# Last two attentions of a four-block kernel: the query projection with tokens on partitions, TensorE turning the result, ScalarE summing the squares

## What is computed

```python
# attention three: 16 query heads, 4 key heads of width 128, queries from x, keys and values from ctx (64 tokens each)
q = rmsnorm(x @ Wq + bq) * qn_w          # per head: q * rsqrt(mean(q*q) + 1e-6)
k = rmsnorm(ctx @ Wk + bk) * kn_w
out = softmax(q @ k.T / sqrt(128) + mask) @ (ctx @ Wv + bv) @ Wo
# attention four: the same heads, keys and values from ctx and x together (128 tokens), rotary positions
q = rope(rmsnorm(x @ Wq.T) * q_norm_w, pos_q)
k = rope(rmsnorm(concat(ctx, x) @ Wk.T) * k_norm_w, pos_k)
out = softmax(q @ k.T / sqrt(128)) @ v @ Wo.T
```

## Time and profile before

| what | value |
|---|---|
| median of three runs | 1300.43 us |
| the profiled execution: time / span | 1304.3 us / 1302.5 us |
| TensorE, VectorE, ScalarE, GpSimd busy | 88%, 65%, 48%, 27% of the span |
| attention three, first projection to the last output projection | 513.5 to about 735 us |
| attention four, the same | 968.9 to about 1222 us |
| share of the chain that ended last: TensorE, VectorE, ScalarE | 65%, 18%, 5% |

### The profile page before, as it was taken

How to read it: one execution, slowest core, us unless ns; L and a number is a source line. 1 busy time by engine, 2 the same in 40 slices (tenths; PEclk the granted TensorE clock), 3 DMA queues, 4 the chain that set the end, 5 groups by cost and what they waited for, 6 DMA issues and landing times.

```text
span 1302.5 us, 22884 instructions
## 1 busy us (share of the span) xinstructions
PE 1147.4 (88%) x8124; PEld 844.3 (65%) x8147; DVE 850.5 (65%) x1920; ACT 621.5 (48%) x1407; POOL 352.9 (27%) x328
## 2 busy tenths in 40 slices
PE   4867869999969999899999988888998999999894
PEld 3554644444455665889988746666657888898753
DVE  7788966888867663455546585333497777775664
ACT  5575435677733343344433422222266766666252
POOL 0040011222121002222222146566422433334032
PEclk8756976999969999899999889899999999999998
DMA  7010034000032235000000262522371000000100
GB/s 257 2 44 1 1 137 203 1 2 2 2 134 91 88 140 174 1 2 1 1 1 1 92 288 84 196 85 86 101 289 66 17 18 17 17 9 9 49 1 33
DMA packets 44571, 89.30 MB, mean 69 GB/s; under 512 B 7280, under 2 KB 30448, under 8 KB 42672
## 3 DMA queue, kind: packets, MB, share of 16 engines
q1 hardware_dynamic: 39184, 73.45, 15.7%
q0 software_dynamic: 5280, 14.42, 3.4%
HBM read 68.72 MB, written 21.10 MB: 69 GB/s over the span
## 4 chain that ended last, share of the span: by engine, by line
PE 65%; DVE 18%; issue 6%; ACT 5%; DMA 2%; POOL 2%; SPq 1%; another core or an unknown queue 1%; DVEq 0%; ACTq 0%; POOLq 0%; PEldq 0%
PE psum L2566 5%; PE psum L2154 4%; PE psum L3183 4%; PE psum L2126 4%; PE psum L3155 3%; PE psum L2586 3%; PE psum L1702 2%; PE psum L1274 2%; PE psum L3056 2%; PE psum L3103 2%; PE psum L2079 2%; PE psum L3125 2%; PE psum L3490 2%; PE psum L2057 2%; PE psum L1720 2%
## 5 line engine op out<-in xcount | busy, mean ns | idle before, releaser
L1469 DVE TENSOR_REDUCE c_max<-psum 128x2 f32<-128x512 f32 x128 | 84.2, 680 | 19.7 <-PE psum L1274 18.2
L1369 ACT ACTIVATE c_probs<-psum 128x512 f32<-128x512 f32 x128 | 75.1, 597 | 35.6 <-PE psum L1285 35.4
L2566 PE MATMUL psum<-m_experts,m_tileT 128*128 x188 | 69.2, 493 | 19.2 <-issue 13.4
L3183 PE MATMUL psum<-a_wo,a_outT 128*128 128x256 f32 x256 | 75.1, 405 | 0.7 <-DVE x_tok L3365 0.7
L2208 ACT ACTIVATE a_probs<-a_probs,a_max 128x64 f32<-128x64 f32 x128 | 42.7, 334 | 44.9 <-DVE a_max L2264 44.9
L3263 ACT ACTIVATE a_probs<-psum,a_max,a_q_rstd 128x128 f32<-128x128 f32 x128 | 56.8, 458 | 11.3 <-DVE a_max L3313 11.2
L2566 PEld LDWEIGHTS psum<-m_experts,m_tileT 128*128 128x128 f32 x188 | 35.8, 199 | 38.6 <-issue 27.9
L2126 PE MATMUL psum<-ctxT_yT_hi,a_wq 128*128 128x128 f32 x256 | 52.9, 290 | 8.2 <-DVE a_qT L2250 7.1
L2875 POOL DMA_INDIRECT m_back<-m_out_tiles,m_rows_of_slots x47 | 46.8, 995 | 46.9 <-DVE m_out_tiles L2809 39.6
L2643 ACT ACTIVATE m_tile_silu<-psum 128x176 f32<-128x176 f32 x47 | 14.9, 318 | 91.0 <-PE psum L2566 56.3
L2250 DVE TENSOR_TENSOR a_qT<-psum,a_columns 128x512 f32<-128x512 f32 x32 | 22.0, 688 | 55.4 <-PE psum L2126 55.4
(11 more groups left out here) (576 smaller groups left out, 3397.6 us busy)
## 6 DMA issues: line engine op xcount, KB each, us to landing
m_w<-m_w SPq DMA_DIRECT2D x8, 1536.0 KB, 14.5
m_experts<-m_e SPq DMA_DIRECT2D x16, 608.0 KB, 12.2
a_wq<-a_wq SPq DMA_DIRECT2D x2, 2048.0 KB
m_rows_back<-m_back SPq DMA_DIRECT2D x4, 1024.0 KB, 8.9
a_ctx_kv<-a_ctx_k_v SPq DMA_DIRECT2D x8, 512.0 KB, 4.3
ctxT_yT_hi<-f_gate_up SPq DMA_DIRECT2D x2, 1024.0 KB
a_v<-a_ctx_kv SPq DMA_DIRECT2D x16, 128.0 KB, 2.7
a_wo<-a_wo SPq DMA_DIRECT2D x1, 2048.0 KB, 7.8
```

What stands on the lines that cost most here:

```text
L1369: e.activation(c1P[:, n % 8, :, :], ps[:, 2 + n % 2, :].rearrange("p (k t) -> p k t", k=2), ACT.Exp, scale=float(1.0 / np.sqrt(np.float32( ...
L1469: e.tensor_reduce(c1M[:, u % 2, j, :], ps[:, c1_score_bank(n), :].rearrange("p (q t) -> p q t", q=2), AX.X, ALU.max).then_inc(c1_mx, 1)
L2566: ins = e.matmul(ps[:, 4 + t % 2, 0:M2_UP], m2xT[:, t % 2, kc, :], m2e[:, bass.ds(own + kc * M2_UP, M2_UP)], start=(kc == 0), stop=(kc == ...
L3183: ins = e.matmul(ps[:, 7, 0:D], a3at[:, i % 2, h, :, :], a3wo[:, h, :], start=(h == 0 and g is None), stop=(h == HQ - 1), skip_group_check ...
```

## The change

For groups in both attentions the operands of the projection are exchanged: 128 tokens are the stationary operand and 512 columns of the weights are streamed, so a group takes two matmuls. The result has tokens on partitions. ScalarE squares each head (128 columns) and sums it with the accumulator, four instructions a group; the matmuls with ones are gone. VectorE gathers the sums in four small instructions a tile, one slot earlier than before (`a2_pair(n, 2)`). TensorE turns the four heads one slot after they were squared (`queries_turned`) and ScalarE copies them into `a_qT`.

In attention three VectorE adds the bias from PSUM into `a_q_tok`, ScalarE squares that copy, and the turned heads have bank 5; the turned keys move to bank 4, which they share with the values. The bias row is loaded over the place of the key weights. In attention four ScalarE reads the projection in PSUM, then VectorE multiplies it with the tables out of the same bank (halves swapped by addressing, two instructions), adds, and TensorE turns the sum back into the same bank: from group 6 on `queries_turned(g)` waits until VectorE has read group g + 1.

The angles and sines of the queries are dropped in the feed-forward stage: queries take theirs from the key tables, in 256-byte pieces.

```diff
@@ -2105,56 +2105,43 @@
                 e.wait_ge(*a2_kn.at(i + 1))
                 if i:
                     e.wait_ge(*a2_kT.at(i))
...
+                    ins = e.transpose(ps[:, 4, j * P:(j + 1) * P], a2kn[:, j * HD:(j + 1) * HD], identf[:, :])
+                ins.then_inc(a2_kTp.sem, 1)
+
+            def value(i):
+                e.wait_ge(*a2_kT.at(i + 1))
                 for kk in range(KC):
 
             def queries(g):
                 i, j = g // 4, g % 4
                 if g:
+                    e.wait_ge(*a2_qb.at(g))
+                for kk in range(KC):
+                    ins = e.matmul(ps[:, 6, :], a2tok[kk][:, 1, i * P:(i + 1) * P], a2wq[:, kk, j * 512:(j + 1) * 512], start=(kk == 0), stop=(kk == KC - 1))
+                ins.then_inc(a2_qp.sem, 1)
...
-
-            def out_and_squares(n):
-
...
-                    e.wait_ge(*a2_o.at(2 * i + 1 + c // 2))
-                    if c == 0 and i:
-                        e.wait_ge(*a2_res.at(i))
-                for k in range(4):
-                    if g is not None:
-                        b2, p_ = k // 2, 2 * (g % 4) + k % 2
-                        at_ = D + (p_ // 4) * 8 + (p_ % 4) * 2 + b2
-                        s_ = b2 * 256 + (k % 2) * P
-                        ins = e.matmul(ps[:, 7, at_:at_ + 1], a2qs[:, g % 4, s_:s_ + P], onesf[:, 0:1], start=(c == 0 and k == 0), stop=True,
-                                       skip_group_check=True)
-                        if k == 3:
-                            ins.then_inc(a2_sp.sem, 1)
-                    if u is not None:
-                        h = 4 * c + k
-                        ins = e.matmul(ps[:, 7, 0:D], a2at[:, i % 2, h, :, :], a2wo[h // 8][:, h % 8, :], start=(h == 0 and g is None), stop=(h == HQ - 1),
-                                       skip_group_check=True)
-                        if h == HQ - 1:
-                            ins.then_inc(a2_wp.sem, 1)
+                    ins = e.transpose(ps[:, 5, h * P:(h + 1) * P], a2qk[:, g % 2, h * HD:(h + 1) * HD], identf[:, :])
+                ins.then_inc(a2_qtp.sem, 1)
+
+            def out_projected(u):
+                i, c = u // 4, u % 4
+                e.wait_ge(*a2_o.at(2 * i + 1 + c // 2))
+                if c == 0 and i:
+                    e.wait_ge(*a2_res.at(i))
+                for h in range(4 * c, 4 * c + 4):
+                    ins = e.matmul(ps[:, 7, 0:D], a2at[:, i % 2, h, :, :], a2wo[h // 8][:, h % 8, :], start=(h == 0), stop=(h == HQ - 1))
+                if c == 3:
+                    ins.then_inc(a2_wp.sem, 1)
...
             def query_squares(g):
-                e.wait_ge(*a2_q.at(g + 1))
-                if g >= 4:
-                    e.wait_ge(*a2_sp.at(g - 3))
-                e.activation(a2qs[:, g % 4, :], a2qT[:, g // 4 % 2, g % 4, :], ACT.Square).then_inc(a2_qf.sem, 1)
+                e.wait_ge(*a2_qb.at(g + 1))
+                if g >= 8:
+                    e.wait_ge(*a2_sr.at(g // 4 - 1))
+                for h in range(4):
+                    c = g % 4 * 4 + h
+                    ins = e.activation(a2qs[:, g % 2, h * HD:(h + 1) * HD], a2qk[:, g % 2, h * HD:(h + 1) * HD], ACT.Square, accum_out=a2qa[:, g // 4 % 2, c:c + 1])
+                ins.then_inc(a2_qf.sem, 1)
+
+            def queriesT(g):
+                i, j = g // 4, g % 4
+                e.wait_ge(*a2_qtp.at(g + 1))
+                if i >= 2:
+                    e.wait_ge(*a2_s.at(2 * (i - 2) + j // 2 + 1))
+                e.activation(a2qT[:, i % 2, j, :].rearrange("p (b h t) -> p b h t", b=2, h=4), ps[:, 5, :].rearrange("p (h b t) -> p b h t", b=2, h=4),
+                             ACT.Copy).then_inc(a2_q.sem, 1)
 
             def probsT(w):
...
                 e.wait_ge(*a2_qp.at(g + 1))
-                if i >= 2:
-                    e.wait_ge(*a2_s.at(2 * (i - 2) + j // 2 + 1))
-                bias = bc(a2c[:, 4 * j:4 * j + 4], 1, 2).unsqueeze(3).broadcast_to([P, 2, 4, S])
-                e.tensor_tensor(a2qT[:, i % 2, j, :].rearrange(v4, b=2, h=4), ps[:, 6, :].rearrange(v4, b=2, h=4), bias, ALU.add).then_inc(a2_q.sem, 1)
+                if g >= 2:
+                    e.wait_ge(*a2_qf.at(g - 1))
+                    e.wait_ge(*a2_qtp.at(g - 1))
+                e.tensor_tensor(a2qk[:, g % 2, :], ps[:, 6, :], a2bq[:, j * 512:(j + 1) * 512], ALU.add).then_inc(a2_qb.sem, 1)
+
...
@@ -3120,7 +3127,7 @@
                 if u:
                     e.wait_ge(*a3_o.at(u))
                 else:
-                    e.wait_ge(*a3_qr.at(A3_LEAD))
+                    e.wait_ge(*a3_q.at(A3_LEAD - 1))
                 for j in range(2):
                     ins = e.matmul(ps[:, 3, j * 256:(j + 1) * 256], a3v[:, i % 2, b2, (2 * hb + j) * HD:(2 * hb + j + 1) * HD], a3pt[:, u % 2, j * 256:(j + 1) * 256],
                                    start=True, stop=True)
+                    e.wait_ge(*a3_qr.at(g))
+                elif g >= 2:
+                    e.wait_ge(*a3_q.at(g - 1))
+                for kk in range(KC):
+                    ins = e.matmul(ps[:, a3_q_bank(g), :], a3tok[kk][:, 1, i * P:(i + 1) * P], a3wq[:, kk, j * 512:(j + 1) * 512],
+                                   start=(kk == 0), stop=(kk == KC - 1))
+                ins.then_inc(a3_qp.sem, 1)
+
+            def queries_turned(g):
+                e.wait_ge(*a3_rot.at(g + 1))
+                e.wait_ge(*a3_qr.at(g + 1 if g < A3_LEAD - 1 else min(g + 2, A3_U)))
+                if g == A3_U - 1:
+                    e.wait_ge(*a3_q.at(g))
                 for h in range(4):
-                    for kk in range(KC):
...
-                    e.wait_ge(*a3_sr.at(min((n + 5) // 4, NT)))
-                if g is not None:
-                    e.wait_ge(*a3_qf.at(g + 1))
-                if u is not None:
-                    i = u // 4
...
+                    ins = e.transpose(ps[:, a3_q_bank(g), h * P:(h + 1) * P], a3rot[:, g % 2, h * HD:(h + 1) * HD], identf[:, :])
+                ins.then_inc(a3_qtp.sem, 1)
+
+            def out_projected(u):
...
 
-            def queries(g):
+            def query_squares(g):
                 e.wait_ge(*a3_qp.at(g + 1))
-                if g >= 4:
-                    e.wait_ge(*a3_sp.at(g - 3))
-                bank = a3_q_bank(g)
-                e.activation(a3qs[:, g % 4, :], ps[:, bank, :], ACT.Square)
-                if g >= 2:
-                    e.wait_ge(*a3_q.at(g - 1))
-                e.activation(a3f[0:64, g % 2, :], ps[64:128, bank, :], ACT.Copy)
-                e.activation(a3f[64:128, g % 2, :], ps[0:64, bank, :], ACT.Copy).then_inc(a3_qf.sem, 1)
+                if g >= 8:
+                    e.wait_ge(*a3_sr.at(g // 4 - 1))
+                for h in range(4):
+                    c = g % 4 * 4 + h
+                    ins = e.activation(a3qs[:, g % 4, h * HD:(h + 1) * HD], ps[:, a3_q_bank(g), h * HD:(h + 1) * HD], ACT.Square, accum_out=a3qa[:, g // 4 % 2, c:c + 1])
+                ins.then_inc(a3_qf.sem, 1)
+
+            def queriesT(g):
+                i, j = g // 4, g % 4
+                e.wait_ge(*a3_qtp.at(g + 1))
+                if i >= 2:
+                    e.wait_ge(*a3_s.at(4 * (i - 2) + 3 + j // 2))
+                e.activation(a3qT[:, i % 2, j, :].rearrange("p (b h t) -> p b h t", b=2, h=4),
+                             ps[:, a3_q_bank(g), :].rearrange("p (h b t) -> p b h t", b=2, h=4), ACT.Copy).then_inc(a3_q.sem, 1)
 
             def probsT(u):
...
             def square_sums(i):
-                e.wait_ge(*a3_sp.at(4 * i + 4))
+                e.wait_ge(*a3_qf.at(4 * i + 4))
                 if i >= 2:
                     e.wait_ge(*a3_rq.at(i - 1))
-                e.tensor_scalar(a3qss[:, i % 2, :], ps[:, 7, D:D + 16], HD * 1e-6, None, ALU.add).then_inc(a3_sr.sem, 1)
+                for odd in range(2):
+                    for b2 in range(2):
+                        ins = e.tensor_scalar(a3qss[S * odd:S * odd + S, i % 2, 8 * b2:8 * b2 + 8], a3qa[S * b2:S * b2 + S, i % 2, odd:16:2], HD * 1e-6, None, ALU.add)
+                ins.then_inc(a3_sr.sem, 1)
 
             def maxima(u):
                 e.wait_ge(*a3_s.at(u + 1))
+            def queries_read(g):
+                i = g // 4
+                raw = ps[:, a3_q_bank(g), :].rearrange("p (h a t) -> p h a t", h=4, a=2)
                 e.wait_ge(*a3_qf.at(g + 1))
                 if g:
-                    e.wait_ge(*a3_q.at(g))
-                e.tensor_tensor(a3t1[:, :].rearrange(v4, b=2, h=4), ps[:, a3_q_bank(g), :].rearrange(v4, b=2, h=4), table(0), ALU.mult).then_inc(a3_qr.sem, 1)
-                dve_step(e, e.tensor_tensor(a3t2[:, :].rearrange(v4, b=2, h=4), a3f[:, g % 2, :].rearrange(v4, b=2, h=4), table(1), ALU.mult))
-                if i >= 2:
-                    e.wait_ge(*a3_s.at(4 * (i - 2) + 3 + j // 2))
-                e.tensor_tensor(a3qT[:, i % 2, j, :], a3t1[:, :], a3t2[:, :], ALU.add).then_inc(a3_q.sem, 1)
+                    e.wait_ge(*a3_rot.at(g))
```

(21 more changed lines are left out.)

237 lines of the change are left out of this document (107 added, 130 removed).

## The result

The changed kernel takes 1323.9 us (median of four runs, 1319.4 to 1327.2) against 1300.3 us for the kernel before, run beside it: a ratio of 1.018, 95% interval 1.015 to 1.021. The forecast was 1320.5 us. The profiled execution took 1319.4 us with a span of 1317.6 us and a mean granted clock of 0.924.

The account below looks back on a forecast made before the run. TensorE was taken to bound the steady parts, until another wait takes its place. Attention four's slots +14.4 and +0.3, its start +10.5, attention three -5: +20 us, 1320.5 us as a median; range 1294 to 1341 us.

Parts of the forecast that it names:

- signs of being wrong: In the profile after: TensorE busy without idle before L3172, or four squares in under 1.2 us.
- The mechanism of attention four: Steady slots: turnings wait until the next group is squared and read in the same bank; 1.22 us a slot, +14.4 us.
- The squares' term: Attention four, ScalarE: four squares with sums take 1.87 us, like four exponentials out of PSUM; bounds 1.2 and 2.7 us.
- milder form of rival (a): Attention four's squares at 1.2 us: chain 2.75 us, a draw; about 1293 us; chance 0.18 together with the full form.
- rival (a): Both attentions: TensorE's work alone counts, about 30 slots of each lose 0.51 us; 1269 us; chance 0.18 with milder form.
- rival (d): Whole kernel: the turned form saves and costs nothing, waits and savings cancel; 1298 to 1303 us; chance 0.05.
- The small additions: Attention four, VectorE: a tile's four small sums just ahead of a reading add 0.3 us in four slots.
- The start of attention four: First fourteen slots: 79.7 us against 71.2, +8.5, and 2 us for the clock: +10.5 us.
- The forecast's terms for ScalarE: Attention four, slots 0 to 6: ScalarE bounds, 6.9 to 7.1 us a slot, 9.0 in slots 0 and 4.
- Attention three: Four steady slots 23.5 us, 1.5 less: -6; slots before +2, end -1; together -5 us.
- Rival (b): Attention four's steady slots: the clock falls there too, in every second of 24 slots; +18 us, 1338 us; chance 0.12.
- The dropped angles and sines: Beside the experts' unbroken TensorE matmuls: priced at nothing; without that cover worth up to 10 us.

Follow-up runs that it names:

- both edits: Changed kernel with attention four's turned queries in bank 2 and its small additions at the end of VectorE's slot: 1263.1 us, 0.9912 of the kernel before.

## Why the prediction was right, and where it was not

The time came within 3.4 us of the forecast. In part that is luck: two terms of attention four were wrong in opposite directions. And one of the prediction's own signs of being wrong came up, four squares in under 1.2 us.

- **The mechanism of attention four was right**: projection, squares and read in one bank, with the turnings behind them, became the path. The waits are at L3172, released by L3335, and go when the turnings get their own bank. GpSimd's power, twice 2.88 us in the chain of attention four's start before, is out of it.
- **The squares' term was mis-sized.** 1.87 us were taken from the exponentials out of PSUM; four squares took 1.14, just under the lower bound of 1.2, which had supposed starts no closer than 0.33 us; they come every 0.25. The chain is 2.70 us instead of 3.42, the wait 0.52 instead of 1.22. With 2.70 the prediction's own sum for four slots (4 x 7.31 + 0.88 + 3.43, each slot 0.72 shorter) is 30.7. Turnings after a wait take 0.63 instead of 0.44 before the next work starts: 31.4, and the kernel with the small additions moved away shows 31.5. That would have been +0.7 us in four slots; that kernel's ratio of 1.0037 is 1305 us, 15 below the forecast, 12 above the milder form of rival (a) and close to rival (d).
- **The small additions were mis-sized the other way.** They were priced at 0.3 us in four slots and cost 2.0 (8.8 less 6.8), because GpSimd holds them up. The prediction took their length from no row beside a working GpSimd; undisturbed in the same place, as reductions, they cost the 0.3. The two errors cancel: 33.5 us measured, 33.9 forecast, and +13.4 us where +14.7 was expected from slot 7 on.
- **The start of attention four** cost 15.6 us and not 10.5: 30.8 us to slot 0 for 27.2, 55.8 us for slots 0 to 6 for 52.5. With both causes taken away (both edits) the start takes 27.3 + 45.9 = 73.2 us, 2.2 more than before. So some 13 of the 15.6 us come from the shared bank and the additions. The forecast's terms for ScalarE, which it took as the bound there, were too long (6.0 to 6.4 us in slots 1, 3 and 5, for 6.9 to 7.1), and the additions missing (10.1 and 11.4 us in slots 2 and 6). The clock may have taken more than the 2 us allowed for, but no run isolates its price: the granted clock is 0.83 until slot 0 and 0.92 in slots 0 to 6, where it was 0.94 and 0.95 before.
- **Attention three** gained 5.7 us in the first profiles (forecast 5) and 4 us by its own ratio. Four steady slots take 23.1 us, against 23.5: the short wait that the forecast put there did not come.
- **Rival (b)** was right as a mechanism and wrong in number. After the additions' long wait of 2.5 us the clock fell once in the steady slots (the same wait in the other turns did not bring it down), and that slot took 10.5 us instead of 8.8, close to the 1.5 us of the earlier trace rows:

```profile
1133.00:1137.00 4.00, 2.28 (x17) 1.82 (x15) 3.78 (x8) 1.74 (x9) 2.69 (x3) 1.00 0.08 27
1137.00:1141.00 4.00, 3.20 (x10) 2.78 (x11) 2.63 (x6) 2.18 (x9) 2.25 (x1) 0.62 0.13 41
```

  Nor did the waits of 0.52 us: the granted clock is 1.00 in the windows of 20 us from 1050 to 1130. With both edits TensorE runs 128 us (1012 to 1140) without idle time, its added turnings in it, at a clock of 1.00. What the Trainium skill, page "TensorE: Matmul & The Clock Gate", section Part 4, says of turnings in transpose mode did not decide here.
- **Rival (a)** is what the kernel with both edits does in the steady slots of attention four. It needed two waits removed, not cheaper squares alone.
- **The dropped angles and sines** were priced at nothing, which no run contradicts: attention three's change alone, which keeps them, begins it at 510.2 us.

## What to carry to other kernels

Work taken off the busiest engine pays only as long as what replaces it does not make a longer chain between engines: here one PSUM bank used for two steps of a pipeline cost 17 to 20 us, more than the change gained in the best of the edited kernels (0.9%, 11 us). Price small operations that stand ahead of a critical read by what runs beside them, not by their length alone; one such group, moved to the end of its engine's slot, gave 14 to 18 us of attention four. And when an engine has time to spare, what new work on it costs is set by what is queued behind it.

## What the runs showed of the hardware that was not expected

- A TENSOR_SCALAR of 64 x 8 elements from SBUF to SBUF on VectorE takes 0.16 us with GpSimd idle and up to 1.0 us when GpSimd runs a TENSOR_TENSOR of 512 columns; it ends when GpSimd's operation does. A SCALAR_TENSOR_TENSOR of 128 x 4 with two inputs from SBUF, 0.16 us otherwise, did so once: with the small additions last it takes 0.57 us from 1076.98 on, beside a GpSimd operation of 1.04 us from 1076.50. A TENSOR_REDUCE of 64 x 8 takes 0.16 us beside GpSimd's TENSOR_TENSORs of 512 columns.
- A Square of 128 columns out of PSUM with its sum starts every 0.25 us (0.28 and 0.21 us long, overlapping), an exponential of the same size with scale and bias from SBUF every 0.43 to 0.45.
- The same kernel before takes 1300 us in some sets of executions and 1273 in others, and both stand on record under one chip number. The attentions take the same time in both; most of the difference lies between them, in the experts, where the changed kernel's TensorE waits 19.3 us before L2572 in one profile and 1.6 in the other. What brings it about is open.
